# Layer 0 of a graph network: linear attention and edge flags split into pieces between stretches of the neighbour aggregation, and a GNN dense stage ordered by column group

## The chip, the core and the metric

One core of a Trainium2 chip runs the whole program as a single launch. The metric is the device time of that core in microseconds (us), the median of the runs given. TensorE is called PE, VectorE DVE, ScalarE ACT, GpSimd POOL and SyncE SP, as in the profile.

## What is computed

3125 nodes with 256 features and 100000 edges pass through two layers. The change is in the first block of layer 0:

```python
xn = _layernorm(x, axis=-1)
x = x + _L0_gnn_ref(xn, src, dst, edge_weight, deg_isqrt[:, None], ...) + _L0_mix_ref(xn[None], W_qkv, W_out, b_out)[0]
# _L0_gnn_ref
agg = segment_sum(edge_vals[:, None] * x[edge_src], edge_dst)
y = agg + eps_weight * x
h = relu(_batchnorm(y @ w1.T, gamma1, beta1))
y = relu(_batchnorm((h @ w2.T) * n_norm, gamma_h, beta_h)) + x
# _L0_mix_ref: q, k, v of 4 heads of 32
k = softmax(k, axis=2)                      # over the nodes
context = einsum('bhld,bhle->bhde', k, v)
out = einsum('bhde,bhld->bhle', context, q) @ W_out + b_out
```

Everything behind it (an expert stage, an edge attention of layer 1, its linear attention and feed-forward stages) stays as it was.

## The kernel before

Nodes lie in 25 tiles of 128 (`NT`). The edges, sorted by target, are cut into 416 items of 256 edges, each within one tile of targets. All of layer 0's first block is two functions, `stage_aggregate` and `stage_gnn0`, each one block with a program per engine; an engine works its program in order, and semaphores are all that ties them together.

**`stage_aggregate`** (from L665). Ahead of the loop, DVE computes the edge flags that layer 1 will read (L853 to L875, stored by SP, L777 to L783), and PE, ACT and DVE work out the linear attention: its keys (seven column groups, L926, kept by L813), their maximum over the nodes (L880), the exponential (L815), then for each of the 25 tiles a transpose (L935), a copy (L821) and a product that sums `exp(k)·xn` (L942), then four small products in a chain (L947 to L957). What is left of the attention is one 256x256 matrix, `c0` (L899), to be multiplied with `xn`.

Then comes a loop of 26 passes with 16 items in each, a `Fori` on POOL, ACT, DVE and PE. For an item POOL gathers two times 128 source rows of `xn` (L802), ACT multiplies them by the edge weights (L827), DVE makes two 128x128 membership matrices (L906), PE multiplies these with the rows into PSUM (L977), and DVE adds the sum to the tile's rows of `acc` (L913) and hands the next index to POOL (L914):

```python
for v in range(0, UI, 4):
    for u in range(v, v + 4):      # two member matrices (L906) for each of four items
    for u in range(v, v + 4):      # value_load of the tile, wait for the sum, acc (L913), index (L914), drain
```

The 16 row buffers form a ring: the gather of an item of the next pass waits for the index that DVE writes after it has added the same item of this pass. Twice a pass PE also projects edge features (16 small products, L969) that ACT copies (L834), SP stores (L773) and for which SP then loads the next features (L767); they stand ahead of items 0 and 8 in PE's order.

**`stage_gnn0`** (from L984). SP loads weights, gains, a bias and `eps` (L1042 to L1048). DVE adds `eps * xn` to `acc` (L1152), PE transposes 25 tiles (L1065, kept by L1124), then turns the degree norms into a row (L1074, kept by L1130), then makes the first product (L1092), whose groups ACT keeps (L1134) and DVE takes statistics of (L1175). ACT applies batch norm and relu (L1143). The second product follows (L1092 again; L1182 and L1185 on DVE), the second batch norm and relu, the product of `c0` with the columns of `xn` (L1104), which DVE adds with the bias (L1192), and 25 transposes back (L1114), which DVE adds to `x` (L1199). PE waits for the `c0` product's additions before it transposes back.

## Time and profile before

| | us |
|---|---|
| median of 3 runs | 4587.69 (4578.02 to 4601.68) |
| the profiled execution's own time | 4554.43 |
| its span, first to last instruction | 4552.7 |
| of it: start of the aggregation's block to the loop | 79.7 to 149.8 |
| loop | 149.8 to 1435 |
| GNN dense stage | 1436 to 1550.5 |
| everything behind it | 1550.5 to 4552.7 |

Busy shares of the span are PE 71%, its weight loads 55%, DVE 49%, POOL 41% and ACT 37%. The profiled execution is 0.7% below the median of the runs. In the profile a float32 matmul is recorded as two MATMUL and two LDWEIGHTS entries, so a group with x50 holds 25 products.

### The profile page before, as it was taken

The numbers are of one execution on the slowest core, as the hardware profiler recorded it, in microseconds if no ns is written. First come the engines' busy times: TensorE is split into PE (matmuls) and PEld (weight loads), VectorE is DVE, ScalarE is ACT, GpSimd is POOL, SyncE is SP. The second block draws the span as 40 slices with busy tenths as digits, with TensorE's granted clock in tenths as the row PEclk, the third lists the DMA queues.
The fourth block names the chain that finished last, engine by engine and source line by source line (L and its number), as shares of the span: only waits on it lengthen the run. The fifth ranks groups of instructions, "written<-read, shape, count | busy, mean of one in ns | idle before, by whom it ended". The sixth has DMA issues, their size and how long they took to land. (4 is left out here: it accounts for less than half of the span.)

```text
span 4552.7 us, 61520 instructions
## 1 busy us (share of the span) xinstructions
PE 3248.1 (71%) x13410; PEld 2514.2 (55%) x13411; DVE 2248.6 (49%) x5291; ACT 1696.8 (37%) x3883; POOL 1863.0 (41%) x1845
## 2 busy tenths in 40 slices
PE   2656565665656779779477777778877777766978
PEld 1445454554545468655356665566665656644656
DVE  6233333333334530074566766677666766664424
ACT  1322322222232212233344555555545545532323
POOL 2566656666663025310235444454544444421010
PEclk8767767777677879889689989988888998877989
DMA  5344444444442036630345555555555555520000
GB/s 140 97 113 112 117 112 117 112 119 115 114 119 54 30 118 218 192 115 38 127 139 163 153 164 161 144 169 161 160 159 152 155 157 160 146 98 20 1 22 29
DMA packets 341326, 545.08 MB, mean 120 GB/s; under 512 B 170239, under 2 KB 221699, under 8 KB 337621
## 3 DMA queue, kind: packets, MB, share of 16 engines
q0 software_dynamic: 113216, 348.74, 27.2%
q1 hardware_dynamic: 220801, 185.13, 14.2%
q10 hardware_dynamic: 7236, 10.35, 0.6%
q8 instruction: 33, 0.54, 0.0%
q14 instruction: 40, 0.33, 0.0%
HBM read 493.32 MB, written 51.90 MB: 120 GB/s over the span
## 5 line engine op out<-in xcount | busy, mean ns | idle before, releaser
L2757 POOL DMA_INDIRECT store<-kv_d,flash_index x832 | 844.5, 1015 | 919.8 <-PE flash_sums L2802 637.6
L802 POOL DMA_INDIRECT agg_rows<-xn_d,agg_index x832 | 800.7, 962 | 542.5 <-DVE agg_index L914 285.0
L977 PE MATMUL agg_sums<-agg_rows,agg_member 128*128 128x257 f32 x1664 | 584.2, 523 | 456.7 <-DVE agg_member L906 248.1
L977 PEld LDWEIGHTS agg_sums<-agg_rows,agg_member 128*128 128x128 f32 x1664 | 441.6, 273 | 594.2 <-issue 277.5
L913 DVE TENSOR_TENSOR acc<-acc,agg_sums 128x257 f32 x416 | 176.4, 424 | 755.8 <-issue 471.5
L2782 PE MATMUL flash_query<-q,flash_mem_t 128*128 x1664 | 438.3, 409 | 51.9 <-DVE store L2990 21.9
L2795 PE MATMUL flash_sums<-store,flash_member 128*128 128x264 f32 x1664 | 441.0, 399 | 6.0 <-DVE store L3055 3.7
L2802 PE MATMUL flash_sums<-acc,ident 128*128 x832 | 282.2, 423 | 211.4 <-issue 147.4
L2782 PEld LDWEIGHTS flash_query<-q,flash_mem_t 128*128 128x128 f32 x1664 | 329.6, 204 | 108.9 <-issue 59.3
L827 ACT ACTIVATE agg_rows<-agg_rows,weight_of 128x256 f32<-128x256 f32 x832 | 341.0, 496 | 77.7 <-DMA agg_rows<-xn_d,agg_index 48.1
L2795 PEld LDWEIGHTS flash_sums<-store,flash_member 128*128 128x128 f32 x1664 | 323.3, 196 | 71.3 <-issue 12.4
L2905 ACT ACTIVATE acc<-flash_sums 128x264 f32 x416 | 159.8, 384 | 537.2 <-remote 289.3
L834 ACT ACTIVATE agg_ep<-agg_edge 128x512 f32<-128x512 f32 x52 | 31.1, 597 | 834.2 <-remote 611.9
L2990 DVE TENSOR_TENSOR store<-store,flash_query 128x1024 f32<-128x1024 f32 x208 | 253.0, 1216 | 158.3 <-remote 114.8
L2802 PEld LDWEIGHTS flash_sums<-acc,ident 128*128 128x128 f32 x832 | 152.7, 200 | 282.6 <-issue 266.0
L2896 ACT ACTIVATE flash_member<-lane,lane_of 128x128 f32<-128x128 f32 x832 | 264.7, 395 | 0.0
L2983 DVE TENSOR_TENSOR store<-store,flash_ep 128x1024 f32<-128x1024 f32 x208 | 252.8, 1216 | 13.8 <-issue 12.9
L3055 DVE TENSOR_TENSOR store<-store,flash_pa 128x1056 f32<-128x1056 f32 x208 | 255.7, 1250 | 0.0
L2994 DVE TENSOR_REDUCE flash_dots<-store 128x32 f32<-128x1024 f32 x208 | 247.9, 1212 | 1.8
L969 PE MATMUL agg_edge<-agg_we,agg_feats 65*128 65x32 f32 x1664 | 205.0, 278 | 50.0 <-issue 47.6
L969 PEld LDWEIGHTS agg_edge<-agg_we,agg_feats 65*128 65x128 f32 x1664 | 208.1, 200 | 42.2 <-issue 39.0
L906 DVE TENSOR_SCALAR agg_member<-lane,lane_of 128x128 f32<-128x128 f32 x832 | 184.0, 302 | 91.0 <-issue 90.4
(473 smaller groups left out, 4806.1 us busy)
## 6 DMA issues: line engine op xcount, KB each, us to landing
moe_w<-in_L_ffn_W_dram SPq DMA_DIRECT2D x64, 512.0 KB
agg_feats<-in_ef_t_dram SPq DMA_DIRECT2D x52, 512.0 KB
flash_goal<-goal_d SPq DMA_DIRECT2D x52, 512.0 KB
agg_rows<-xn_d,agg_index POOLq DMA_INDIRECT x832
ep_d<-agg_ep SPq DMA_DIRECT2D x52, 256.0 KB
store<-kv_d,flash_index POOLq DMA_INDIRECT x832
flash_ep<-ep_d SPq DMA_DIRECT2D x416, 32.0 KB
flash_flags<-flags_d SPq DMA_DIRECT2D x416, 32.0 KB
```

Source lines behind the costliest of these rows:

```text
L802: pool.indirect_dma_start(rows[:, q, 0:D], None, sh.xn_d, bass.IndirectOffsetOnAxis(ap=index[:, q:q + 1], axis=0)).then_inc(gathered[u], 16)
L827: act.activation(rows[:, q, 0:D], rows[:, q, 0:D], ACT.Copy, scale=sh.weight_of[:, bass.ds((UI * i + u) * SUBS + k, 1)]).then_inc(weighted, 1)
L969: last = pe.matmul(edge[:, c * DH:(c + 1) * DH], feats[:, c * P:(c + 1) * P], we_s[:, :], start=True, stop=True)
L977: last = pe.matmul(sums[:, u % 4, 0:W], member[:, u % WI * SUBS + k, :], rows[:, q, :], start=(k == 0), stop=(k == SUBS - 1))
L2757: pool.indirect_dma_start(ring[:, s, :], None, sh.kv_d, bass.IndirectOffsetOnAxis(ap=index[:, s:s + 1], axis=0)).then_inc(gathered[p][g], 16)
L2782: last = pe.matmul(query[:, c * D:(c + 1) * D], mem_t[:, g % 2, c * P:(c + 1) * P], sh.q[:, bass.ds(t, 1), :], start=True, stop=True)
L2795: pe.matmul(sums[:, n % 3, 0:W], member[:, g % 2, c, :], ring[:, a.side * WS + 4 * g + c, HI_], start=(k == 0), stop=False)
L2802: pe.matmul(sums[:, n % 3, 0:W], sh.ident[:, :], sh.acc[:, bass.ds(tiles[n], 1), :, :].rearrange("p a h v -> p (a h v)"), start=False, sto ...
L2896: act.activation(member[:, g % 2, k, :], sh.lane[:, :], ACT.Abs, scale=-1.0, bias=sh.lane_of[:, bass.ds(WS * a.at + (4 * g + k), 1)])
L2983: dve.tensor_tensor(r, r, ep[:, s.side, 4 * g:4 * g + 4, :].unsqueeze(2).to_broadcast([P, 4, H, DH]), ALU.add).then_inc(add_done, 1)
L2990: dve.tensor_tensor(r, r, query[:, :].rearrange("p (k f) -> p k f", k=4), ALU.mult).then_inc(mult_done, 1)
L3055: dve.tensor_tensor(r, r, e.unsqueeze(3).to_broadcast([P, 4, H, VW]), ALU.mult).then_inc(pv_ready, 1)
```

## The change

The loop of 26 passes becomes stretches, with other work between them. Each engine has its own list of passes at which it leaves the loop; POOL keeps a single loop of 26.

```diff
@@ stage_aggregate
+        KEYS_AT, ZSUM_AT, C0_AT = 2, 5, 8
+        FLAGS_AT, FLAGS_OUT_AT = (10, 13), (11, 14)
+        MIX_AT = (13, 15, 17, 19, 21, NI // UI)
+        MIX_TILES = NT // (len(MIX_AT) - 1)
@@ sync: eps, we, be and the first features stand first; the GNN stage's loads are here too
+                sp.dma_start(eps_s[:, :], eps_w.partition_broadcast(P)).then_inc(eps_in, 16)
...
+                feats_load(0)
+                sp.dma_start(b_row[:, :], b_out).then_inc(mix_loaded, 16)
+                for to, of in gnn0_loads:
+                    sp.dma_start(to, of).then_inc(sh.gnn0_in, 16)
@@ scalar
+                items(0, KEYS_AT)
                 for g, (c, w) in enumerate(COLS):
...
+                items(KEYS_AT, ZSUM_AT)
                 for t in range(NT):
...
+                items(ZSUM_AT, FLAGS_OUT_AT[0])
+                act.wait_ge(flags_ready, 1)
+                act.dma_start(flags_half(0), ...).then_inc(flags_out, 16)
+                items(FLAGS_OUT_AT[0], FLAGS_OUT_AT[1])
...
+                items(FLAGS_OUT_AT[1], NI // UI)
@@ vector: acc starts as eps * xn, no longer as zero
-                dve.memset(sh.acc_rows[:, :, 0:W], 0.0)
+                dve.memset(sh.acc_rows[:, :, D:W], 0.0)
+                dve.tensor_scalar(sh.acc_rows[:, :, 0:D], sh.xn[:, :, :], eps_s[:, 0:1], None, ALU.mult)
+                items(0, KEYS_AT)
...
+                items(KEYS_AT, C0_AT)
...
+                items(C0_AT, FLAGS_AT[0])
+                half_flags(0)
+                items(FLAGS_AT[0], FLAGS_AT[1])
+                half_flags(1)
...
+                for n in range(len(MIX_AT) - 1):
+                    for t in range(MIX_TILES * n, MIX_TILES * (n + 1)):
+                        dve.wait_ge(mixed, t + 1)
+                        dve.tensor_tensor(sh.x[0:w, t, :], sh.x[0:w, t, :], keys[0:w, t % 2, 0:D], ALU.add
+                                          ).then_inc(mix_added, 1)
+                    items(MIX_AT[n], MIX_AT[n + 1])
@@ tensor: leaves the loop at passes 2, 5, 8, 13, 15, 17, 19 and 21
+                for n in range(len(MIX_AT) - 1):
+                    for t in range(MIX_TILES * n, MIX_TILES * (n + 1)):
+                        if t >= 2:
+                            pe.wait_ge(mix_added, t - 1)
+                        for k in range(KB):
+                            pe.matmul(keys[:, t % 2, 0:D], sh.xt[:, k, t * P:(t + 1) * P], sh.c0[:, k, :], ...)
+                        pe.matmul(keys[:, t % 2, 0:D], sh.ones[0:1, :], b_row[:, :], ...).then_inc(mixed, 1)
+                    items(MIX_AT[n], MIX_AT[n + 1])
@@ stage_gnn0: no loads, no eps addition, no product of c0, four row banks for two
+                turn(0)
+                for g in range(NG):
+                    if g + 1 < NG:
+                        turn(g + 1)
+                    product(0, g, yt)
+                for g in range(4):
+                    norms(g)
+                for g in range(NG):
+                    product(1, g, ht)
+                    if 1 <= g and g + 3 < NG:
+                        norms(g + 3)
@@ the norm row is kept by DVE, group by group, just ahead of its use
+                    dve.tensor_copy(norm_row[:, c:c + w], row[:, g % 4, 0:w]).then_inc(row_kept, 1)
```

PE's order at the start of the aggregation's block. Before:

```order
L918 UNCONDITIONAL_BRANCH
L926 MATMUL agg_keys<-store,agg_mix_wk 128x512 x12
L926 MATMUL agg_keys<-store,agg_mix_wk 128x53 x2
L935 MATMUL agg_keys<-ident,agg_mix_kt 128x128 x2
L942 MATMUL agg_zsum<-store,agg_mix_ke 128x256
```

Now the loop's first stretch stands there, and the keys follow after its jump back:

```order
L967 COMPARE_AND_BRANCH
L995 MATMUL agg_keys<-store,agg_mix_wk 128x512 x12
L995 MATMUL agg_keys<-store,agg_mix_wk 128x53 x2
L967 UNCONDITIONAL_BRANCH
L967 ISA
L972 ISA
L974 MATMUL agg_edge<-agg_we,agg_feats 128x32 x16
```

The 25 pairs of transpose and product come one stretch later, the four small products another stretch later.

PE's order in `stage_gnn0`, from its first instruction. Before:

```order
L1057 UNCONDITIONAL_BRANCH
L1065 MATMUL gnn_bank<-ident,acc 128x128 x50
L1074 MATMUL gnn_row<-ident,gnn_norm 128x128 x25
L1092 MATMUL gnn_bank<-gnn_yt,gnn_w 128x512 x24
L1092 MATMUL gnn_bank<-gnn_yt,gnn_w 128x53 x4
L1092 MATMUL gnn_bank<-gnn_ht,gnn_w 128x512 x24
L1092 MATMUL gnn_bank<-gnn_ht,gnn_w 128x53 x4
L1104 MATMUL gnn_bank<-store,c 128x512 x24
L1104 MATMUL gnn_bank<-store,c 128x53 x4
L1114 MATMUL gnn_row<-ident,gnn_yt 128x128 x48
```

Now:

```order
L1108 UNCONDITIONAL_BRANCH
L1116 MATMUL gnn_row<-ident,acc 128x128 x16
L1134 MATMUL gnn_bank<-gnn_yt,gnn_w 128x512 x4
L1116 MATMUL gnn_row<-ident,acc 128x128 x8
...
L1134 MATMUL gnn_bank<-gnn_yt,gnn_w 128x53 x4
L1123 MATMUL gnn_row<-ident,gnn_norm 128x128 x16
L1134 MATMUL gnn_bank<-gnn_ht,gnn_w 128x512 x8
L1123 MATMUL gnn_row<-ident,gnn_norm 128x128 x4
...
L1134 MATMUL gnn_bank<-gnn_ht,gnn_w 128x53 x4
L1162 MATMUL gnn_row<-ident,gnn_yt 128x128 x48
```

The transposes alternate with the first product, the norm row stands behind it, and the product of `c0` is gone. Its row form is inside the loop, five times (the first of the five is shown, between two stretches):

```order
L967 COMPARE_AND_BRANCH
L1040 MATMUL agg_keys<-c,store 128x256 x2
L1042 MATMUL agg_keys<-agg_mix_b,ones 128x256
...
L967 UNCONDITIONAL_BRANCH
L967 ISA
L972 ISA
L974 MATMUL agg_edge<-agg_we,agg_feats 128x32 x16
```

Five such pairs of rows stand in each of the five places.

## Rows read from the trace of the kernel before

**Rows 1.** Busy us: PE, PEld, DVE, ACT, POOL; granted clock, DMA share, GB/s, mid-loop

```profile
600.00:800.00 200.00, 119.09 (x499) 99.25 (x498) 62.66 (x253) 56.30 (x136) 121.89 (x127) 0.72 0.44 115
```

**Rows 2.** The page, costliest groups: busy, mean ns | idle before, releaser

```profile
L802 POOL DMA_INDIRECT agg_rows<-xn_d,agg_index x832 | 800.7, 962 | 542.5 <-DVE agg_index L914 285.0
L977 PE MATMUL agg_sums<-agg_rows,agg_member 128*128 128x257 f32 x1664 | 584.2, 523 | 456.7 <-DVE agg_member L906 248.1
```

**Rows 3.** Timeline, DVE's first and last addition of pass 0, first of pass 1

```profile
155.54 0.42 DVE L913 TENSOR_TENSOR acc<-acc,agg_sums 128x257 f32 x1 [3.25 <-PE agg_sums L977]
...
197.10 0.42 DVE L913 TENSOR_TENSOR acc<-acc,agg_sums 128x257 f32 x1 [0.91 <-issue]
...
205.56 0.42 DVE L913 TENSOR_TENSOR acc<-acc,agg_sums 128x257 f32 x1 [5.58 <-remote]
```

**Rows 4.** Timeline, DVE's additions inside a pass: last of item 7, items 8 and 10

```profile
626.74 0.42 DVE L913 TENSOR_TENSOR acc<-acc,agg_sums 128x257 f32 x1 [0.91 <-issue]
...
630.07 0.42 DVE L913 TENSOR_TENSOR acc<-acc,agg_sums 128x257 f32 x1 [0.97 <-issue]
...
640.47 0.42 DVE L913 TENSOR_TENSOR acc<-acc,agg_sums 128x257 f32 x1 [6.81 <-remote]
```

**Rows 5.** Timeline, start of the aggregation's block to the loop's first product

```profile
79.69 0.40 SPq L746 DMA_DIRECT2D agg_mix_wk<-in_L_mix_Wk_dram  x1
...
83.91 13.21 PE L926 MATMUL agg_keys<-store,agg_mix_wk 128*128 128x512 f32 x28 [5.27 <-DMA agg_mix_wo<-in_L_mix_W_out_dram]
...
89.56 0.68 DVE L857 TENSOR_TENSOR agg_flags<-agg_key 104x508 f32<-104x508 f32 x1 [0.46 <-issue]
...
92.17 1.29 DVE L865 TENSOR_SCALAR agg_flags<-agg_flags 104x2048 f32<-104x2048 f32 x1
...
105.17 3.34 DVE L880 TENSOR_REDUCE agg_mix_top<-agg_mix_kt 128x1 f32<-128x3125 f32 x1
...
111.83 0.69 PE L935 MATMUL agg_keys<-ident,agg_mix_kt 128*128 128x128 f32 x2 [14.71 <-ACT agg_mix_kt L815]
```

**Rows 6.** Timeline, the 25 tiles of the key sum and the small chain

```profile
126.92 1.22 PE L942 MATMUL agg_zsum<-store,agg_mix_ke 128*128 128x256 f32 x2 [1.40 <-ACT agg_mix_ke L821]
...
129.78 1.22 PE L942 MATMUL agg_zsum<-store,agg_mix_ke 128*128 128x256 f32 x2 [1.42 <-issue]
...
141.49 0.69 PE L942 MATMUL agg_zsum<-store,agg_mix_ke 128*128 128x256 f32 x2
...
143.30 1.23 PE L942 MATMUL agg_zsum<-store,agg_mix_ke 128*128 128x256 f32 x4
...
149.84 3.68 PE L969 MATMUL agg_edge<-agg_we,agg_feats 65*128 65x32 f32 x32
```

**Rows 7.** Timeline, the GNN dense stage

```profile
1439.23 0.43 SPq L1048 DMA_DIRECT2D gnn_eps<-in_L_gnn_eps_weight_dram  x1
1441.83 2.67 DVE L1149 TENSOR_SCALAR gnn_degree<-acc 128x25 f32<-128x25 f32 x1 [6.45 <-DMA gnn_eps<-in_L_gnn_eps_weight_dram]
...
1465.57 21.59 PE L1092 MATMUL gnn_bank<-gnn_yt,gnn_w 128*128 128x512 f32 x56
...
1515.99 21.70 PE L1104 MATMUL gnn_bank<-store,c 128*128 128x512 f32 x56 [1.16 <-DVE gnn_yt L1182]
...
1518.23 9.22 ACT L1143 ACTIVATE gnn_yt<-gnn_yt,gnn_b,gnn_a 128x512 f32<-128x512 f32 x14 [0.94 <-DVE gnn_b L1170]
...
1537.52 0.62 PE L1114 MATMUL gnn_row<-ident,gnn_yt 128*128 128x128 f32 x4
...
1550.11 0.41 DVE L1199 TENSOR_TENSOR store<-store,gnn_row 53x256 f32<-53x256 f32 x1 [0.24 <-PE gnn_row L1114]
```

**Rows 8.** Groups of the GNN dense stage: busy, mean ns | idle before, releaser

```profile
L1065 PE MATMUL gnn_bank<-ident,acc 128*128 128x128 f32 x50 | 9.6, 369 | 16.2 <-DVE acc L1152 16.2
...
L1182 DVE TENSOR_TENSOR gnn_yt<-gnn_bank,gnn_norm_row 128x512 f32<-128x512 f32 (+1 forms) x14 | 8.7, 621 | 8.5 <-PE gnn_bank L1092 8.5
...
L1074 PE MATMUL gnn_row<-ident,gnn_norm 128*128 128x128 f32 x50 | 5.9, 278 | 0.0
```

More of the change, by code:

```diff
@@ L807, in _, with items @@
             def _(act):
+                def items(first_i, end_i):
+                    with act.Fori(first_i, end_i) as i:
+                        for u in range(UI):
+                            hold(act, gathered[u], 16 * SUBS * i + 16 * SUBS, act_ticks)
+                            for k in range(SUBS):
+                                q = u * SUBS + k
+                                act.activation(rows[:, q, 0:D], rows[:, q, 0:D], ACT.Copy,
+                                               scale=sh.weight_of[:, bass.ds((UI * i + u) * SUBS + k, 1)]
+                                               ).then_inc(weighted, 1)
+                            if u % WI == WI - 1:
+                                p = u // WI
+                                act.wait_ge(edge_ready, 2 * i + (p + 1))
+                                act.wait_ge(ep_out[p], 16 * i + 16)
+                                act.activation(ep[:, p, :], edge[:, :], ACT.Copy).then_inc(ep_ready, 1)
                 act.sem_inc(ep_out[0], 16)
@@ new lines, in _ @@
+                dve.tensor_tensor(single[:, :], k0[:, :], k1[:, :], ALU.not_equal)
+                dve.tensor_copy(steps[:, 4 * WS:4 * WS + 1], first[:, :])
+                dve.drain()
+                for n in range(2):
+                    dve.tensor_tensor(steps[:, (2 * n + 1) * WS:(2 * n + 2) * WS], steps[:, 2 * n * WS:(2 * n + 1) * WS],
+                                      single[:, :], ALU.max)
+                dve.drain()
+                dve.tensor_scalar(steps[:, 0:4 * WS], steps[:, 0:4 * WS], -BIG, None, ALU.mult).then_inc(flags_ready, 1)
@@ L918, in _, with items @@
+                for n in range(len(MIX_AT) - 1):
+                    for t in range(MIX_TILES * n, MIX_TILES * (n + 1)):
+                        w = min(P, N - t * P)
+                        dve.wait_ge(mixed, t + 1)
+                        dve.tensor_tensor(sh.x[0:w, t, :], sh.x[0:w, t, :], keys[0:w, t % 2, 0:D], ALU.add
+                                          ).then_inc(mix_added, 1)
+                    items(MIX_AT[n], MIX_AT[n + 1])
             @block.tensor
             def _(pe):
+                def items(first_i, end_i):
+                    with pe.Fori(first_i, end_i) as i:
+                        for u in range(UI):
+                            if u % WI == 0:
+                                p = u // WI
+                                pe.wait_ge(feats_in, 32 * i + (16 * p + 16))
+                                pe.wait_ge(ep_ready, 2 * i + (p + 1))
+                                for c in range(WS):
+                                    last = pe.matmul(edge[:, c * DH:(c + 1) * DH], feats[:, c * P:(c + 1) * P],
+                                                     we_s[:, :], start=True, stop=True)
+                                last.then_inc(edge_ready, 1)
+                            pe.wait_ge(added, UI * i + (u + 1))
+                            for k in range(SUBS):
+                                q = u * SUBS + k
+                                pe.wait_ge(weighted, NB * i + (q + 1))
+                                pe.wait_ge(member_ready, NB * i + (q + 1))
+                                last = pe.matmul(sums[:, u % 4, 0:W], member[:, u % WI * SUBS + k, :], rows[:, q, :],
+                                                 start=(k == 0), stop=(k == SUBS - 1))
+                            last.then_inc(summed, 1)
@@ L944, in _ @@
                     last.then_inc(pe_small, 1)
+                items(ZSUM_AT, C0_AT)
                 pe.wait_ge(dve_small, 1)
@@ L1070, in _, with turn @@
-                for g, (c, w) in enumerate(COLS):
-                    if g >= 2:
-                        pe.wait_ge(row_kept, g - 1)
-                    for t in range(c // P, -(-(c + w) // P)):
-                        last = pe.matmul(row[:, g % 2, t * P - c:t * P - c + P],
+                def turn(g):
+                    for t in tiles_of(g):
+                        if t >= 4:
+                            pe.wait_ge(turn_kept, t - 3)
+                        for k in range(KB):
+                            last = pe.transpose(row[:, t % 4, k * P:(k + 1) * P], sh.acc_rows[:, t, k * P:(k + 1) * P],
+                                                sh.ident[:, :])
+                        last.then_inc(turn_ready, 1)
```

313 lines of the change are left out of this document (129 added, 184 removed).

## The prediction

> **What bounds the kernel now.** I read the windows first, then the page's costliest groups, then the timeline of the three places that change: the start of the aggregation's block, one pass of its loop, the GNN dense stage. Nothing behind 1550.5 us is touched.
>
> In the loop no engine is full: in 200 us PE is busy 119, POOL 122, DVE 63, ACT 56, at a mean granted clock of 0.72, so between the levels of 1.2 and 2.4 GHz [rows 1]. The 26 passes take 1285 us, 49.4 each. POOL could do its 32 gathers of a pass in about 40 (each starts 1.26 us after the last while it streams, the 0.96 of the page and 0.30 between), but it stands idle 542.5 us ahead of its gathers over the whole program, 285.0 of them until DVE hands over an index, and PE waits for DVE's membership matrices [rows 2]. So the loop is a ring POOL, ACT, PE, DVE, POOL with little left over, and work put into PE's order between two passes mostly lengthens it. The start of the block is plain serial time: the first order goes out at 79.69, the loop's first edge product runs at 149.84 [rows 5, 6]. In the dense stage PE runs one long group after another, with a late start [rows 7].
>
> **One more thing in the loop.** DVE's last addition of pass 0 starts at 197.10 and its first of pass 1 at 205.56, 8.5 us later [rows 3]; between the other passes this is mostly 8 to 10. The same change of items inside a pass, with the same edge products on PE between them, takes 3.3 us, 626.74 to 630.07 [rows 4]. So about 5.2 us per jump are a hold-up that belongs to no engine's work. Similar ones stand inside a pass: DVE idles 6.81 us ahead of the addition at 640.47 [rows 4]. There are some three per pass, and they come while gathers stream.
>
> **Part by part, against the profiled execution** (span 4552.7, its own time 4554.43, which is 33.3 us or 0.7% below the median of 4587.69).
>
> 1. *The loop starts at once.* Now SP has four short orders and a register load ahead of the first features: about 79.7 + 2.6 = 82.3. The small load of rows 7 took 2.6 us from issue to release (1439.23 to 1441.83); 512 KB at the loop's 115 GB/s [rows 1] add 4.6, so 89.5. DVE meanwhile needs some 3 us of clearing and an `eps * xn` over 6400 elements; at 1.29 us for 2048 [rows 5] that is 4.0, so about 88. First edge product at 89, not 149.8: **-61**. Bounds: -52, if the long DVE operation goes at the pace of the old fused addition, and -63.
> 2. *GNN dense stage.* The eps addition and the loads ahead of it are gone, and 25 transposed tiles (9.6 us of PE [rows 8]) alternate with the first product (21.6 [rows 7]): both end at 1436.4 + 31.2 = 1467.6, where the first product ended at 1487.2: -19.6. The norm row costs PE 0.24 us per tile [rows 8], sixteen tiles beside the coefficients and nine among the second product: +2. DVE now also keeps the row, 7 x 0.6 us, but in the second product it idled 8.5 us for PE [rows 8], so that is hidden. The product of `c0` (21.7 us on PE) held the transposes back until 1537.5; now they wait only for the relus, which begin at 1518.2 and take 0.34 us per tile (9.22 for all, [rows 7]). Back transposes from 1519.6 at the old pace, 12.6 us for 25 [rows 7], end at 1532.2 for 1550.5: -18.3. Sum **-36**, bounds -28 and -38.
> 3. *Keys, maximum, exponential* between passes 1 and 2: 13.2 us on PE, then 6.7 from the start of the maximum to the first transpose [rows 5], less the 3.7 us of edge products that PE can do in that wait: **+17**, bounds 10 and 24. ACT is held for all of it and weights nothing.
> 4. *Key sum*, 25 tiles. With no gathers running a tile took 0.6 us (141.49 to 143.30 is three); while gathers streamed, 2.86 (126.92 to 129.78) [rows 6]. When PE and DVE stand, POOL runs out of indices after some 7 us (an estimate: six gathers of 1.26 us, for the three items that DVE frees last), so three slow tiles and 22 quick ones: **+22**, bounds 15 and 71.
> 5. *Small chain*: from the end of the key sum, 143.30 + 1.23, to the edges at 149.84 it is 5.3, and leaving the loop costs a little: **+6** [rows 6], bounds 4 and 8.
> 6. *Flags*: a half takes 4 us of DVE (89.56 to the end of the 1.29 at 92.17 [rows 5]), the steps 1. PE's edge products run beside it, so little is seen: **+3**, bounds 0 and 9. The flag stores go to ACT's queue, two passes ahead of the wait for the first; no stall.
> 7. *The product of c0 in rows*: 75 products of 256 columns in five places. A product of 257 columns took 0.70 us in the loop (584.2 / 1664 x 2 [rows 2]), 2.1 per tile, 10.5 per place. DVE's addition of 0.4 lies beside the next tile. **+53**, bounds 32 (all at full clock, half of the 0.86 that 512 columns take in rows 7) and 75. This is more than the 18 it saves in part 2; only the sum with part 1 pays.
> 8. *What the pauses swallow.* At eight places PE leaves the loop. POOL's stream ends in the pause, and DVE does not jump back, so the 5.2 us hold-up can fall into it: between 0 and 8 x 5.2 = 42. I take three quarters, **-31**, since each pause is longer than the hold-up, but after the row products DVE starts its matrices only when PE is free.
>
> Sum: -61 - 36 + 17 + 22 + 6 + 3 + 53 - 31 = **-27**. Against the median, 4587.7 - 27 = 4561 us. It lies near the limit of what a measurement here can tell from no change, 0.5% or 23 us.
>
> **A rule against the trace.** What the rows show is 8.5 us across the jump against 3.3 us inside a pass [rows 3, 4]. If that hold-up comes with the jump alone, all eight go and part 8 is -42. The Trainium skill, page "Runtime: NRT & Kernel Launch", section "Instruction fetch mechanics", says that a taken branch to code outside the two pages in reach stops the engine until the target is fetched. By that rule alone the sum is -38; the trace agrees in that the hold-up recurs at the jump, but similar ones stand in mid-pass, where no jump is, so it is not the whole of it.
>
> **The rivals.**
>
> - *All hold-ups at the jumps vanish*: -38, 4550 us. For it: the regular 8.5 us. Against: the mid-pass hold-ups. The fetch rule above is this rival's.
> - *The loop has slack for the pauses.* POOL needs 40.3 of 49.4 us per pass. If POOL's filling of the ring during a pause lets PE and DVE run the next pass faster by 5 us on top of part 8, eight or nine places give 45: -72, 4516. For it: POOL idles 542.5 us. Against: the first pass of the old loop, entered with a full ring, was no quicker inside: 155.54 to 197.10 is 41.6 us [rows 3], and 49.4 - 8.5 = 40.9 is the usual.
> - *Nothing is swallowed*: the hold-ups only move. Part 8 is 0, the sum +4: 4592, no change. A dense stage that does not reach the 36 comes to the same.
> - *Slower: inline code beside streaming gathers is served slowly.* The place is PE's and ACT's straight runs between stretches. All 25 tiles of the key sum at 2.86 make 71 for 22 (+49), and 25 row tiles at 2.86 for 2.1 add 19: -27 + 68 = +41, 4629. It decides from about 50 us of such extra, that is when nearly all the 25 key tiles are slow. For it: the 2.86 of rows 6 lasted some 17 us. Against: POOL ran for 40 us there because its ring was empty of work done; in the loop it stops much earlier.
>
> **How the numbers follow.** Chances: forecast 0.38 (4545 to 4578 by the bounds of parts 1, 6 and 7 taken together), all hold-ups vanish 0.15, slack 0.15, nothing swallowed 0.14, slower 0.18. The forecast's own range straddles the 0.5% limit at 4565; 0.23 of it is faster, 0.15 is not. Faster: 0.23 + 0.15 + 0.15 = 0.53; same: 0.15 + 0.14 = 0.29, slightly more for a slower rival that only half happens: 0.30; slower 0.17. The range leaves out the outer part of the two extreme cases: 4515 to 4612.
>
> **What would show it.** Part 1: first edge product near 89 us. Part 2: last addition to `x` some 79 us after the last addition to `acc` where it was 115. Part 3 to 7: distances between the additions on both sides of each place, less the usual 8.5: 17, 22, 6, 3 and 10.5. Part 8: whether these distances contain a hold-up. The row tiles' own matmuls must be near 0.35 us per record; at 0.2 the forecast is too high by 21. The prediction is wrong if the stretches' passes are no longer 49 us but, say, 45 or 55, since nothing in my sum changes the pass itself.

## The result, and the profile after

Beside the kernel before, in the same session: **4634.6 us** (median of 4, 4624.6 to 4645.0) against 4586.9 (median of 4, 4578.0 to 4601.7), a ratio of 1.010, 95% interval 1.006 to 1.014. The change is 27 to 65 us slower. The forecast was 4561, with a range to 4612.

The profiled execution took 4644.98 us, with a span of 4643.2; of before it was 4554.43 and 4552.7, below every timed run. So the two profiles lie 90 us apart where the medians lie 48.

**The page.** These answer to [rows 2]; the columns are the same.

```profile
L812 POOL DMA_INDIRECT agg_rows<-xn_d,agg_index x832 | 797.1, 958 | 640.2 <-DVE agg_index L878 387.8
L982 PE MATMUL agg_sums<-agg_rows,agg_member 128*128 128x257 f32 x1664 | 593.3, 528 | 483.7 <-DVE agg_member L870 291.5
```

The work of a gather and of a product is what it was. POOL waits 103 us longer for an index from DVE (387.8 for 285.0): the ring is interrupted, and POOL does not make up for it.

**The start of the block**, timelines of the changed kernel (start, us; engine; in brackets what it idled for). It answers to [rows 5, 6].

```profile
88.13 7.03 PE L974 MATMUL agg_edge<-agg_we,agg_feats 65*128 65x32 f32 x32 [9.69 <-issue]
...
107.10 0.59 PE L982 MATMUL agg_sums<-agg_rows,agg_member 128*128 128x257 f32 x1 [2.26 <-issue]
133.19 6.14 PE L982 MATMUL agg_sums<-agg_rows,agg_member 128*128 128x257 f32 x16 [25.50 <-ACT agg_rows L825]
...
126.97 0.42 DVE L877 TENSOR_TENSOR acc<-acc,agg_sums 128x257 f32 x1 [34.81 <-remote]
...
102.86 0.91 ACT L825 ACTIVATE agg_rows<-agg_rows,weight_of 128x256 f32<-128x256 f32 x2 [0.74 <-issue]
126.90 0.60 ACT L832 ACTIVATE agg_ep<-agg_edge 128x512 f32<-128x512 f32 x1 [23.13 <-remote]
```

The edge product starts at 88.1, as forecast (89). Then the first sums are there, and ACT and DVE do nothing for 23 and 35 us, on a "remote" releaser, and go on together at 126.9. POOL meanwhile sends gathers without a break, the last ending at 121.0.

**What they waited for.** "remote" only says that the semaphore was raised at a time at which no instruction ended. The trace also keeps when each semaphore was raised. ACT waits for `edge_ready`, which the last edge product gives: that product ends at 95.2, and the semaphore is raised at 126.78. DVE waits for `summed`: PE's first four sums end between 97.0 and 107.7, and their four updates come at 126.84, 126.90, 126.96 and 127.02. So the work was done and its signal came up to 31.6 us late. The forecast's distance from the first edge product to the first addition, 5.7 us before (149.84 to 155.54), is now 38.8.

**A place with row tiles**, ahead of pass 15:

```profile
930.42 1.03 PE L1040 MATMUL agg_keys<-c,store 128*128 128x256 f32 x4
931.38 0.69 PE L1042 MATMUL agg_keys<-agg_mix_b,ones 1*128 1x256 f32 x2
...
938.74 1.65 PE L1040 MATMUL agg_keys<-c,store 128*128 128x256 f32 x3 [4.99 <-DVE store L959]
...
941.89 2.08 PE L1040 MATMUL agg_keys<-c,store 128*128 128x256 f32 x4
943.90 1.22 PE L1042 MATMUL agg_keys<-agg_mix_b,ones 1*128 1x256 f32 x2
...
948.20 7.04 PE L974 MATMUL agg_edge<-agg_we,agg_feats 65*128 65x32 f32 x32
...
930.86 0.42 DVE L877 TENSOR_TENSOR acc<-acc,agg_sums 128x257 f32 x1 [0.90 <-PE agg_sums L982]
...
938.27 0.42 DVE L959 TENSOR_TENSOR store<-store,agg_keys 128x256 f32<-128x256 f32 x1 [6.91 <-remote]
```

Two tiles come at full speed. DVE adds the first of them only at 938.27, held 6.91 us, so PE, with two banks for these tiles, waits. Here too the signal is late: the first tile's product ends at 932.07 and its semaphore `mixed` is raised at 938.25. All 25 updates of `mixed` are in the trace; the first tile's comes 7.6, 6.2, 9.5 and 3.3 us late at the places 13, 15, 17 and 21, and 0.01 us late at 19. What follows a late one is at half speed: 2.08 + 1.22 us for the first tile's 1.03 + 0.69, the edges 7.04 us for 3.7.

**The dense stage**, timelines (answers to [rows 7]):

```profile
1535.23 1.04 PE L1116 MATMUL gnn_row<-ident,acc 128*128 128x128 f32 x8
...
1528.77 0.42 DVE L877 TENSOR_TENSOR acc<-acc,agg_sums 128x257 f32 x1 [0.91 <-PE agg_sums L982]
...
1592.67 7.71 DVE L1240 TENSOR_TENSOR store<-store,gnn_row 128x256 f32<-128x256 f32 x21 [2.40 <-PE gnn_row L1162]
...
1590.31 9.22 ACT L1193 ACTIVATE gnn_yt<-gnn_yt,gnn_b,gnn_a 128x512 f32<-128x512 f32 x14 [0.94 <-DVE gnn_b L1216]
...
1591.97 8.95 PE L1162 MATMUL gnn_row<-ident,gnn_yt 128*128 128x128 f32 x50 [5.38 <-ACT gnn_yt L1193]
...
1602.78 3.37 DVE L614 BATCH_NORM_STATS2 n_stats<-store 128x6 f32<-128x256 f32 x10 [1.08 <-PEq L73]
```

The back transposes follow the relus at once, 1.66 us behind their start.

**The ledger** on which the rest is told. *Start* to *norm* are from DVE's timeline: *start* is its first addition to `acc`; *loop* from there to its last one; *dense* from there to the first instruction of the norm behind the stage; *norm* is when that starts. "Later" is the part of the later attention from its first gather to its last, which no kernel here touches.

| kernel | start | loop | dense | norm | later |
|---|---|---|---|---|---|
| before | 155.5 | 1279.3 | 116.4 | 1551.3 | 1762.3 |
| changed | 127.0 | 1401.8 | 74.0 | 1602.8 | 1804.4 |

So 51 of the 90 us between the profiles arise in the changed block. The later attention is 42 us longer, and what is left is 3 us shorter.

### The profile page after: what moved, and what is told of

Its sections match the earlier page's. It is cut to its first block and busy times, and to the rows that moved or that the text cites. A ratio compares the mean times of both kernels' runs of the same rounds, so it can differ in the third digit from the quotient of the medians.

```text
span 4643.2 us, 61715 instructions
## 1 busy us (share of the span) xinstructions
PE 3322.6 (72%) x13504; PEld 2570.5 (55%) x13505; DVE 2242.4 (48%) x5305; ACT 1695.6 (37%) x3876; POOL 1851.4 (40%) x1845
## 5 line engine op out<-in xcount | busy, mean ns | idle before, releaser
L812 POOL DMA_INDIRECT agg_rows<-xn_d,agg_index x832 | 797.1, 958 | 640.2 <-DVE agg_index L878 387.8
L2836 PEld LDWEIGHTS flash_sums<-store,flash_member 128*128 128x128 f32 x1664 | 329.5, 200 | 77.4 <-issue 16.2
L974 PE MATMUL agg_edge<-agg_we,agg_feats 65*128 65x32 f32 x1664 | 226.8, 297 | 32.3 <-issue 30.2
L974 PEld LDWEIGHTS agg_edge<-agg_we,agg_feats 65*128 65x128 f32 x1664 | 228.4, 219 | 36.0 <-issue 33.3
```

What stands on the lines that cost most here:

```text
L812: pool.indirect_dma_start(rows[:, q, 0:D], None, sh.xn_d, bass.IndirectOffsetOnAxis(ap=index[:, q:q + 1], axis=0)).then_inc(gathered[u], 16)
L974: last = pe.matmul(edge[:, c * DH:(c + 1) * DH], feats[:, c * P:(c + 1) * P], we_s[:, :], start=True, stop=True)
L2836: pe.matmul(sums[:, n % 3, 0:W], member[:, g % 2, c, :], ring[:, a.side * WS + 4 * g + c, HI_], start=(k == 0), stop=False)
```

## The experiments

Eighteen kernels ran, in five sessions; with that of the result there are six. They met chips of two plainly different kinds, which must be known to read the numbers. In four of the six (that of the result, e1 to e4, e13 to e16, e17 and e18) the kernel before takes 4587 to 4621 us; in the other two (e5 to e8, e9 to e12) it takes 3812 and 3817. I call them **slow and fast chips**. Every ratio below is against the kernel before on the same chip.

| run | chip | start | loop | dense | norm | later | ratio, 95% interval |
|---|---|---|---|---|---|---|---|
| e1 rows out | slow | 127.6 | 1346.5 | 95.2 | 1569.4 | 1782.9 | 0.997, 0.994 to 1.000 |
| e2 one place | slow | 127.4 | 1420.7 | 77.0 | 1625.1 | 1815.5 | 1.008, 1.006 to 1.011 |
| e3 start 8 | slow | 105.2 | 1418.7 | 73.9 | 1597.9 | 1797.7 | 1.003, 1.000 to 1.007 |
| e4 before, depth 8 | slow | 144.6 | 1305.3 | 117.5 | 1567.5 | 1770.1 | 0.998, 0.995 to 1.001 |
| e5 filler | fast | 96.2 | 1046.3 | 74.1 | 1216.5 | 1291.7 | 0.981, 0.980 to 0.983 |
| e6 before, split | fast | 144.4 | 1018.1 | 116.7 | 1279.2 | 1291.0 | 0.999, 0.998 to 1.000 |
| e7 ahead of loop | fast | 142.7 | 1021.7 | 95.2 | 1259.6 | 1298.3 | 0.994, 0.992 to 0.996 |
| e8 before | fast | 144.8 | 1018.7 | 116.0 | 1279.5 | 1296.3 | one run |
| e9 changed | fast | 96.8 | 1049.1 | 77.1 | 1223.0 | 1291.7 | 0.982, 0.980 to 0.984 |
| e10 filler | fast | 97.0 | 1048.0 | 75.4 | 1220.4 | 1292.7 | 0.983, 0.981 to 0.984 |
| e11 ahead of loop | fast | 142.8 | 1021.3 | 92.1 | 1256.2 | 1297.3 | 0.994, 0.993 to 0.996 |
| e12 ahead, start 8 | fast | 141.8 | 1034.5 | 95.3 | 1271.6 | 1293.0 | 0.996, 0.995 to 0.998 |
| e13 before, split | slow | 164.2 | 1302.8 | 116.3 | 1583.3 | 1769.6 | 1.001, 0.998 to 1.004 |
| e14 filler | slow | 127.0 | 1400.3 | 76.7 | 1604.0 | 1781.5 | 1.008, 1.006 to 1.010 |
| e15 ahead of loop | slow | 163.5 | 1305.9 | 95.4 | 1564.7 | 1801.9 | 0.995, 0.992 to 0.997 |
| e16 before | slow | 162.2 | 1306.6 | 117.2 | 1586.0 | 1800.3 | one run |
| e17 rows out | slow | 126.8 | 1353.9 | 92.1 | 1572.9 | 1818.0 | 0.998, 0.995 to 1.001 |
| e18 before, pauses | slow | 159.8 | 1429.4 | 117.2 | 1706.4 | 1796.8 | 1.035, 1.029 to 1.041 |

### e1 and e17: the rows out of the loop

```
-        MIX_AT = (13, 15, 17, 19, 21, NI // UI)
-        MIX_TILES = NT // (len(MIX_AT) - 1)
+        MIX_AT = (13, NI // UI)
+        MIX_TILES = 0
...
+                for g, (c, w) in enumerate(COLS):
+                    for m in range(KB):
...
+                            last = pe.matmul(bank[:, q % 4, 0:w], sh.c0[:, k, m * P:(m + 1) * P],
+                                             sh.xt[:, k, c:c + w], start=(k == 0), stop=(k == KB - 1))
```

(with DVE's addition of bias and product, in the form of the kernel before).

> The changed kernel with its row product taken out of the loop: no row tiles and no row adds at the places 13 to 21, and the product c0 by xt added by columns in the dense stage again, in the form of the kernel before, behind the second product's normalisation (14 products, 14 scalar_tensor_tensor). Theory A (the five places cost what the gaps between the aggregation's adds show, +79 us over the usual 8.5 us between passes; the dense stage gets some 22 us back): the gaps at 13, 15, 17, 19 and 21 fall to 8 to 10 us, the norm behind the block starts near 1546 instead of 1602.8, and the time is near 4578, at or below the kernel before. Theory B (the loop's passes are slower for another reason, its instructions being in eight loops, and the gaps would open elsewhere): gaps or passes stay long, and the time stays above 4610.

> As e1_rows_out (on a slow chip 0.997 of the kernel before): linear attention and flags in the loop, c0's product in columns in the dense stage, no row tiles. On a slow chip again 0.993 to 1.000. On a fast chip: the first add at 97, the loop some 1030 to 1035 us (keys, key sum and chain each a gap of 18 to 19 us where the usual is 10 to 12), the dense stage 95 us, the norm behind near 1225 to 1230 as in the changed kernel, ratio 0.982 to 0.988: what the rows cost in the loop, 15 us, and what they save in the dense stage, 20 us, nearly cancel there.

The ratios are 0.997 and 0.998, near the kernel before. The rows cost 52 us of loop (1401.8 against the mean 1350.2 of these two) and save 20 us of the dense stage. By the gaps alone (from the last addition of a pass to the first of the next) they seemed to cost 79 us; but with the rows out the passes themselves got longer, so part of a hold-up does fall into a stop. The norm starts at 1569 and 1573, not at 1546: the loop is still some 50 us longer than before's, from keys, key sum, chain and flags. That part of the expectation failed.

### e2: all rows at one place

```
+        MIX_AT = (13, NI // UI)
+        MIX_TILES = NT
```

> The changed kernel with all 25 row tiles at one place, ahead of pass 13, instead of five at each of five. If the stop is what costs (the adds' engine late by 3 to 9 us at each place, then cold clock): one late start of about 9 us, 25 tiles at 1.7 to 2 us each, one edge product, together 50 to 60 us over the usual gap where five places have 79, so the time is 20 to 30 us below the changed kernel, near 4610. If the tile is what costs (3.15 us each with TensorE at its lower clock): 25 x 3.15 = 79 us at the one place, and the time is the changed kernel's, 4635.

Nothing won: the one gap has 89.8 us, 81 above the usual 8.5, and the ratio is 1.008. PE's timeline there:

```profile
815.08 1.02 PE L1040 MATMUL agg_keys<-c,store 128*128 128x256 f32 x4
816.03 0.69 PE L1042 MATMUL agg_keys<-agg_mix_b,ones 1*128 1x256 f32 x2
...
827.63 2.07 PE L1040 MATMUL agg_keys<-c,store 128*128 128x256 f32 x4 [9.22 <-DVE store L959]
829.64 1.22 PE L1042 MATMUL agg_keys<-agg_mix_b,ones 1*128 1x256 f32 x2
...
897.00 2.08 PE L1040 MATMUL agg_keys<-c,store 128*128 128x256 f32 x4
...
900.16 7.04 PE L974 MATMUL agg_edge<-agg_we,agg_feats 65*128 65x32 f32 x32
```

Behind a wait of 9.22 us every tile takes 3.15 us for the 1.7 of the first two. The window from 828 to 897 us (columns as [rows 1]) shows PE busy throughout at a granted clock of 0.50, the level of 1.2 GHz:

```profile
828.00:897.00 69.00, 69.00 (x132) 36.42 (x131) 8.84 (x21) 0.00 (x0) 0.00 (x0) 0.50 0.00 0
```

So 69 us of unbroken work did not bring the clock back. Theory "the tile costs" came, with 81 us for 79: what costs is the tile at the low clock, not the number of stops.

### e5, e10 and e14: PE kept busy in the wait

Twelve products that nobody reads, 6.1 us at full clock:

```
+                        if t % MIX_TILES == 2:
+                            for _ in range(12):
+                                pe.matmul(zsum[:, 0:D], sh.ident[:, :], sh.xt[:, 0, 0:D], start=True, stop=True)
                         if t >= 2:
                             pe.wait_ge(mix_added, t - 1)
```

> The changed kernel with twelve matrix products of 128x128 by 128x256 that nobody reads (into the key sum's bank, free by then) put on TensorE behind the first two row tiles of each place, 6.1 us at full clock. Theory A (at the places 13, 15, 17 and 21 TensorE idles 6 to 9 us for the first row add, its clock falls, and the other tiles and the edge products run at 1.2 GHz): with the idle time filled the clock stays, row tiles stand 1.7 us apart and the next edge product takes 3.7 us; the gaps go from 25 to 28 us to some 18 to 20, place 19 gets 6 us longer, and the norm behind the block comes some 25 us earlier, time near 4610. Theory B (the clock would fall in any case): tiles stay at 3.15 us, every gap grows by 6 to 10 us more, and the time is 4665 or more.

> As e5_filler, now beside the changed kernel on one chip. Theory A on a slow chip: four of five gaps 7 to 10 us shorter than the changed kernel's, time 15 to 35 us below it. On a fast chip, where VectorE is not held up, TensorE does not idle at the places and the filler is 6 us of work at each: 0 to 10 us above the changed kernel, as POOL's gathers cover most. Theory B: 30 us above it on a slow chip.

> As e10_filler_again, which on the fast chip made no difference to the changed kernel (3750 against 3748). On a slow chip, theory A (TensorE idles for the late first row add and loses its clock): the gaps at 13, 15, 17 and 21 fall from 25 to 28 us to about 18, place 19's grows to 21, ratio to the kernel before 1.003 to 1.007 where the changed kernel has 1.010. Theory B: gaps of 30 us or more and a ratio of 1.015 or more.

On the slow chip, ahead of pass 15:

```profile
935.04 5.23 PE L1039 MATMUL agg_zsum<-store,ident 128*128 128x256 f32 x23
...
940.33 1.03 PE L1043 MATMUL agg_keys<-c,store 128*128 128x256 f32 x4
941.28 0.69 PE L1045 MATMUL agg_keys<-agg_mix_b,ones 1*128 1x256 f32 x2
...
945.28 4.69 PE L974 MATMUL agg_edge<-agg_we,agg_feats 65*128 65x32 f32 x32
```

The mechanism is as thought: where the filler covers the wait, the tiles stay at 1.7 us, and the gaps at 13, 15 and 17 are 19.6, 13.4 and 14.6 us for 26.8, 26.4 and 28.1. At 19 and 21 the signals were later than the filler lasts (up to 9.6 us), and the gaps are 25.2 and 26.8 for 15.6 and 24.7. But nothing of it arrives: the loop has 1400.3 us for 1401.8. The passes inside took 1089 us in sum where the changed kernel's took 1070. The ratio is 1.008, where theory A had 1.003 to 1.007; the result's 1.010 is from another chip, and the two intervals overlap. I count no gain, and why the won gaps are lost again in the passes is not shown. On fast chips filler and changed kernel are alike (0.983 and 0.982 in one session), as expected there.

### e3 and e4: a shorter first run of gathers

```
-                dve.sem_inc(index_ready, UI)
+                dve.sem_inc(index_ready, UI // 2)
```

(e3 in the changed kernel, with the other half given behind pass 1; e4 in the kernel before, for the whole loop.)

> The changed kernel with POOL's first run of gathers halved: it is given 8 items (16 gathers) at the start instead of 16 items (32), the other 8 at the end of pass 1. Theory A (the other engines' work at the start is held until POOL's unbroken run of gathers ends, 32 gathers from 81 to 121 us and first add at 127): the run ends near 101, the first add comes at 105 to 110, the edge product's copy by ScalarE too. Later passes as in the changed kernel, so up to 17 us less: 4618 to 4635. Theory B (the start is held by something of a fixed time, loads of code or weights, and not by POOL's run): the first add stays at 125 to 128 and the time is 4635 or more.

> The kernel before with POOL allowed 8 items ahead instead of 16, in the whole loop; nothing else changed. Theory A (while POOL issues gathers without a break the other engines are held up 5 to 6 us, about three times a pass, until shortly after it stops): its runs are at most 16 gathers, the hold-ups are shorter, a pass takes 44 to 48 us instead of 49.4, and the time falls by up to 100 us, to 4490 to 4560. Theory B (the hold-ups are the loop's jump and do not know of POOL; POOL's lead hides the gathers' latency): passes stay at 49.4 or grow by a few us, 4587 to 4650.

Timelines of e3 (POOL's last gather of its first run, the next one, ACT's copy of the edges, DVE's first addition):

```profile
100.41 0.95 POOL L812 DMA_INDIRECT agg_rows<-xn_d,agg_index  x1 [0.30 <-issue]
106.54 0.95 POOL L812 DMA_INDIRECT agg_rows<-xn_d,agg_index  x1 [5.18 <-DVE agg_index L878]
...
105.18 0.60 ACT L832 ACTIVATE agg_ep<-agg_edge 128x512 f32<-128x512 f32 x1 [0.93 <-remote]
...
105.25 0.42 DVE L877 TENSOR_TENSOR acc<-acc,agg_sums 128x257 f32 x1 [12.58 <-PE agg_sums L983]
```

Halving POOL's first run brings the first addition from 127.0 to 105.2, inside the expected 105 to 110. So the hold-up at the start depends on the length of POOL's run: the late `edge_ready` now comes at 105.06, 10.1 us behind its product. Of these 22 us the loop gives 17 back: the gap at the keys is 31.2 us for 19.6. e4 starts 11 us earlier than the first profile of before, but its passes do not get shorter (expected 44 to 48 us; the loop is 1305.3 us); its 0.998 is no difference.

### e18: pauses in POOL's runs

```
+                        if u % 8 == 7:
+                            for _ in range(7):
+                                pool.memset(rest[:, :], 0.0)
+                                pool.drain()
```

> The kernel before with POOL made to pause some 4 us (seven memsets of a tile that nobody reads, each waited for) behind every 16 gathers. Theory A on a slow chip (the other engines are held up while POOL issues without a break, and released some 6 us behind its last gather): a release behind every 16 gathers, first add at 145 to 152 instead of 155 to 162, and the loop not much longer, 1290 to 1340, though POOL has 8 us more per pass; ScalarE's and VectorE's waits without a releaser get shorter. Rival (the hold-ups don't know of POOL): the first add stays at 155 to 162, and the loop grows by what POOL's pauses add, 30 us or more. On a fast chip, where POOL's 32 gathers fill the 40 us of a pass, the loop grows by some 8 us a pass, 200 us in all.

The rival's numbers came: start at 159.8, loop 1429, ratio 1.035. POOL's first pause lasts from 111.6 to 118.1 us. ACT's waits of the profile from 300 to 700 us:

```profile
ACT agg_ep L839 <- remote: 297.8, 14, 27.2
```

That is more than the 210.6 us in ten waits of the kernel before (e16, below), not less. The signals are no better either: 49 of the loop's 52 updates of `edge_ready` come over 2 us behind the end of their product, the median 11 us. So "POOL's unbroken issuing" is not the cause as I had put it; e3 and e4 changed also how many gathers are under way ahead of the others. What delays the signals stays open.

### e6 and e13: cuts with nothing between

```
-                with dve.Fori(0, NI // UI) as i:
+                cuts = (0, 2, 8, 10, 13, 15, 17, 19, 21, NI // UI)
+                for n in range(len(cuts) - 1):
+                    with dve.Fori(cuts[n], cuts[n + 1]) as i:
```

(the like on ACT and PE.)

> The kernel before, only its aggregation loop written as several loops on ScalarE, VectorE and TensorE, cut where the changed kernel cuts, and nothing put between them. Theory A (a stop costs by what it computes and by the engine that is held up there, a cut by itself is free): gaps stay near 8.5 us everywhere and the time is that of the kernel before within 10 us. Theory B (code met for the first time costs, each cut adds a fetch of new code): gaps or the passes behind the cuts grow by 3 to 8 us at nine cuts, and the time rises by 25 to 60 us.

> As e6_split, of which the fast chip said: cuts by themselves are free (the norm behind at 1279.2 against 1279.5). On a slow chip, theory A: free there too, within 10 us of the kernel before. Theory B: the first time through new code costs there, 3 to 8 us at each of nine cuts, 25 to 60 us in all.

Theory A on both kinds: 0.999 and 1.001. New copies of the loop's code cost nothing that shows. The DMA queues say the same. Of the kernel before, from 190 to 1420 us, which holds every jump of the loop:

```profile
q0 software_dynamic: 37344, 102.02, 30.2%
q1 hardware_dynamic: 54880, 38.54, 13.2%
```

and of e6, from 170 to 1150 us, beside its gathers and loads:

```profile
q8 instruction: 11, 0.18, 0.1%
q14 instruction: 17, 0.14, 0.1%
```

So in the kernel before no packet of code moves during the loop, and the 28 that the cuts bring are not seen in the time.

### e7, e11, e12 and e15: the linear attention ahead of the loop

```
-        KEYS_AT, ZSUM_AT, C0_AT = 2, 5, 8
+        KEYS_AT, ZSUM_AT, C0_AT = 0, 0, 0
```

on top of e1, with stretches of no passes left out. e12 gives POOL 8 items first, the others at the loop.

> The version of e1_rows_out with the whole linear attention (keys, softmax, key sum, chain) ahead of the loop as in the kernel before; the flags' halves stay in the loop and the dense stage stays group by group, with c0's product in columns. In e1_rows_out the pieces cost +67 us in the loop against 28 us that the earlier start gave. Theory A: first add near 148 (VectorE reaches the maximum some 7 us earlier without the flags), the loop some 1285 us, the dense stage 95 us, so the norm behind starts near 1530, 20 us ahead of the kernel before, and the time is 0.3 to 0.7% below the kernel before. Rival (the pieces are paid ahead of the loop as much as within): the norm starts near 1569 as in e1_rows_out.

> As e7_before_loop, which was 0.62% faster than the kernel before on the fast chip, by the dense stage's 21 us alone (1279.5 to 1259.6 at the norm behind). On a slow chip: first add near 148, loop 1285, dense 95, time 15 to 30 us below the kernel before and 50 to 70 us below the changed kernel. On a fast chip as in e7, and slower than the changed kernel.

> e11 with POOL given 8 items at the start and the other 8 when VectorE enters the loop. In e4_depth8 the shorter run of gathers brought the first add from 155.5 to 144.6. Theory A on a slow chip: first add 8 to 15 us earlier than e11's, and half or more of it kept at the norm behind; on a fast chip no gain, 0 to 10 us later there, since POOL, which is the bound, starts its second 16 gathers late. Rival: the catch-up run of gathers holds the others up by as much as was won, no difference on a slow chip.

> As e11_before_loop_again, 0.6% faster than the kernel before on the fast chip. On a slow chip: first add near 148, loop within 10 us of the kernel before's, dense stage 95, ratio 0.993 to 0.997. Rival (pieces are paid ahead of the loop as within, or what they leave is given back in the loop): ratio 1.0 or above.

The ratio is 0.995 on the slow kind of chip and 0.994 on the fast kind: this form keeps the regrouped dense stage (21 us) and the flags in the loop, and is 0.5 to 0.6% below the kernel before on both kinds, with both intervals below 1. On the slow chip its first addition comes at 163.5, not 148, so the flags were not what held the front there; the norm starts at 1564.7 for 1586.0 in e16. e12 met the fast kind only, where it is 7 us slower than e11.

### e8, e9 and e16: the two kernels again

> The kernel before once more, unchanged, for a second profile of it: the first one was of an execution of 4554.4 us, below the lowest of the timed runs. If the difference lies in the loop, its 26 passes take 10 to 30 us longer than 1279; if in the later attention's loop, that one takes longer than 1762.

> The changed kernel itself, beside the kernel before on this chip. The second call fell on a chip on which the kernel before takes 3812 us and a pass 40 us without the hold-ups, where the first chips show 4587 to 4598 us and 50 us a pass. Theory: on a chip of the slow kind the change is 0.6 to 1.4% slower, as shown; on one of the fast kind the first add comes at 96, the loop is some 35 us longer, the dense stage 42 us shorter, and the change is 1.2 to 1.8% faster, 3745 to 3765 against 3812. Rival (the change costs the same everywhere): 0.5% slower or more on either.

> The kernel before once more, for a second profile on this chip. On a slow chip the loop from first to last add takes 1290 to 1310 us (the first profile, of an execution of 4554 us where the timed ones took 4578 to 4602, has 1279.3) and the later attention's gathers 1775 to 1800 (1762.3 there).

**On a fast chip the change is 1.8% faster.** The same code, 3748 against 3817 us, as e9 expected; its rival, the same cost everywhere, failed. e16 shows how before's first profile stands: its loop of 1279.3 us was a short one, e16 has 1306.6. e8 fell on a fast chip and can't tell this.

Waits of ACT and the windows from 300 to 700 us, kernel before, slow chip (e16; waits: us in total, times, longest; windows as [rows 1]):

```profile
ACT agg_ep L834 <- remote: 210.6, 10, 24.4
ACT agg_ep L834 <- PE agg_edge L969: 61.0, 6, 12.5
...
ACT agg_rows L827 <- DMA agg_rows<-xn_d,agg_index: 10.5, 6, 3.4
```

```profile
300.00:700.00 400.00, 244.67 (x1019) 201.86 (x1017) 122.35 (x497) 111.67 (x270) 240.60 (x252) 0.71 0.43 114
```

and on a fast chip (e8):

```profile
ACT agg_rows L827 <- DMA agg_rows<-xn_d,agg_index: 245.6, 125, 6.1
```

```profile
300.00:700.00 400.00, 294.79 (x1261) 252.49 (x1261) 150.93 (x636) 150.48 (x336) 303.41 (x317) 0.78 0.57 143
```

On the fast chip ACT waits for the gathers to land, POOL sends 317 gathers in 400 us, one per 1.26, and POOL is the bound. On the slow chip ACT waits for `edge_ready` instead, ten of the 16 times with a releaser that the profile can't name, and POOL sends 252. Not all of the 210.6 us is lost, since ACT has time to spare; the 65 missing gathers show what is.

The semaphores show why. In e8 all 416 updates of `summed` and all 52 of `edge_ready` come within 0.02 us of the end of the product that gives them. On slow chips many records of `summed` are missing, but those of `edge_ready` are complete in e3, e4 and e14: of 52 updates 26, 24 and 23 come over 2 us late, the latest 31.5 us. For every run I counted the products of the loop that give a signal and have it recorded within 0.2 us of their end: 99% or more on the fast kind of chip, 42 to 51% on the slow kind. Behind the later attention, where nothing is gathered, it is all of them on both kinds. So late signals beside gathers are what sets the slow kind apart. What in the chip delays them is not shown.

In e9 the row tiles ahead of pass 15 meet no hold-up, and all 25 updates of `mixed` come within 0.02 us:

```profile
705.26 0.93 DVE L959 TENSOR_TENSOR store<-store,agg_keys 128x256 f32<-128x256 f32 x2 [0.25 <-issue]
```

```profile
709.11 1.13 PE L1040 MATMUL agg_keys<-c,store 128*128 128x256 f32 x4
...
710.80 3.94 PE L974 MATMUL agg_edge<-agg_we,agg_feats 65*128 65x32 f32 x32
```

and POOL goes on gathering through them, one per 1.26 us, which is why the gaps there (12.2 to 12.6 us at four of the five places) are those of the kernel before on that chip. At place 13 the gap is 24.5 us even so: DVE works on the second half of the flags from 617.1 to 621.8 before it adds the first tile, PE waits 5.3 us, and its tiles then take 3.15 us.

## Why the prediction was wrong

For the slow chips, take before's loop and start as the means of its two profiles and e13, whose cuts cost nothing: 1296 and 161. Then the sum reads:

| part | forecast | measured | how |
|---|---|---|---|
| 1 start | -61 | -34 | 127.0 - 161 |
| 3 to 6 pieces | +48 | +54 | 1350.2 (e1, e17) - 1296 |
| 7 rows | +53 | +52 | 1401.8 - 1350.2 |
| 8 swallowed | -31 | in the two above | |
| 2 dense | -36 | -43 | 74.0 - 116.6 |
| sum | -27 | +29 | |

+29 lies within the 27 to 65 us of the timed runs, near the lower end; what lies between it and 48 is not placed. It depends on the profile taken for before: with the first alone it is +51, with e16 alone +17, so the row of parts 3 to 6 is known to some 20 us only. The later attention's own length goes from 1762 to 1818 us over the slow profiles, with no order among kernels, so nothing behind the block can be read as an effect.

- **Part 1 failed, by 27 us.** The edge product came at 88.1 for 89. But I took everything behind it for running at once, and the signals of PE's first products came up to 31.6 us late, so that the first addition stood 38.8 us behind the edge product for 5.7 to 8.9 in the kernel before. The front of the kernel before had shown what happens beside streaming gathers: tiles of 2.86 us instead of 0.6 [rows 6]. I used that for the key sum, and not for the loop's own first sums. e3, with POOL's run halved, takes 22 us of it away. On the fast chip there is none: the first addition stands 9.1 us behind the edge product in e9, for 8.9 in e8, and the part is -48, since the edge product of e8 came at 135.9 and not at 149.8.
- **Part 8 failed: next to nothing of its 31 us shows in the sum.** Parts 3 to 8 were to make +70 and made +106. In the gaps of the changed kernel there are at the keys 19.6 us, the key sum 25.3, the chain 17.0 and the rows 26.8, 26.4, 28.1, 15.6, 24.7; with the usual 8.5 taken off, the pieces are 11, 17, 8.5 and 79 in sum for the rows, 115 together where the forecast had 98. About 10 of the 115 is won back in the passes (the rows' net 52 for 79 is the plainest case), but the sizes of parts 3 to 7, which I had summed without hold-ups, came out near the net ones, so that nothing was left for part 8 to take off. How the 36 us too few divide between parts 3 to 7 and part 8 is a matter of booking; together they failed by that. The rival "nothing is swallowed" came nearest. With part 1's 27 us it gives 4 + 27 = +31.
- **Parts 3 to 7 held in their net sum, partly by luck.** +106 together for +101. Part 7's net 52 for 53 came from other terms: up to 3.15 us per tile at four places and 1.68 at the fifth, with TensorE waiting in between for late signals, less what the passes gave back, where I had 2.1 throughout. The terms of part 3 as written (13.2 + 6.7 - 3.7) add to 16.2, not 17. The passes themselves stayed as forecast, 41.1 us from first to last addition for 41.7.
- **Part 2 was under-sized**, 43 for 36: four transposed tiles take 1.04 us beside the first product, and the back transposes 8.95 us in all for 12.6.
- **The rival on the slower side** had the right sign and size (+41) and the wrong place. Its condition, a slow key sum, did not occur: the sum took some 17 us at its place. Slow service beside gathers struck at the start and at DVE's first addition of four of the five row places.
- **The fetch rule.** The 8.5 us from the last addition of a pass to the first of the next [rows 3] are no fixed price of the jump: on the fast chip the early passes of before have 5.7. Nor are they fetches: no packet of code moves in the loop of the kernel before, and e6 and e13, where some do, lose nothing. That rule (the Trainium skill, page "Runtime: NRT & Kernel Launch", section "Instruction fetch mechanics") would have made these cuts dearer or the stops cheaper; the traces here show neither.
- **The rival "the loop has slack"** (-72, 1.6%) has the number of the fast chip, but not its mechanism: measured 1.8% faster, start -48, loop +30, dense -39 there. On it the passes did not get shorter (788 us in sum from first to last addition for 771); POOL is the bound and goes on during the stops. The trace of before could not tell that such chips exist.

## What to carry to other kernels

Work put between passes of a loop is near free only where the bound engine goes on through the stop; look for that in the trace (POOL at one gather per 1.26 us), not for idle shares. For a wait without a named releaser ("remote"), look when the work was done and when its semaphore was raised; such a wait must be priced again wherever its circumstances return, here gathers in a long run. A piece of TensorE work split over stops here ran at half clock when both of its banks waited for the consumer; more banks might help, which no run tried. Time such a change on more than one chip: this one is 1.0% slower on some and 1.8% faster on others, and the version with the linear attention ahead of the loop, the flags in it and the regrouped dense stage is 0.5 to 0.6% faster on both kinds.

## What the runs showed of the hardware

- Two kinds of chip: the same program took 4587 to 4621 us in four sessions and 3812 and 3817 in two. The difference is in the two loops fed by gathers (the first 1279 to 1307 us against 1019, the later attention 1762 to 1818 against 1291 to 1298); the parts between take 681 to 691 us everywhere.
- On the slow kind the semaphore updates of PE come late beside gathers: up to 31.6 us behind the end of the product at the loop's start (95.2 to 126.78), 3.3 to 9.5 us at four of the five row places. On the fast kind all 416 sums of e8 signal within 0.02 us. ACT and DVE stand for that long, up to 23 and 35 us at the start. Pauses of 6 to 7 us after each 16 gathers did not help (e18). What delays the updates is not shown.
- TensorE's clock fell to 1.2 GHz behind waits of 5 to 9 us and stayed there (granted 0.50) through 69 us of back-to-back products (e2). Twelve products that nobody reads, put in the wait, kept the tiles at the pace of 2.4 GHz at three of five places (e14).
- The loop of the kernel before fetches no code: no `instruction` packet from 190 to 1420 us. The 28 such packets in e6's loop cost nothing measurable (0.999).
